# An attention and expert block on one core: tiles normalised inside the attention steps, and linear-attention states added from PSUM

## The reference

```python
xn = layernorm(x)
q, k, v = xn @ Wq, xn @ Wk, xn @ Wv          # 16 heads of 16
# heads 0..3: softmax attention over the own window of 128 tokens and the one before it, causal
# heads 4..15: linear attention, in blocks of 64 tokens
q = softmax(q); k = elu(k) + 1
ctx = cumsum(k^T v over blocks) / (cumsum(sum of k) + 1e-6)     # of the blocks before
out = q @ ctx
attn = concat(local, out) @ Wo + bo
# experts: 8 of them, each token goes to the two with the best scores xn @ router_w.T
h = gelu(xn @ w1[e].T); y += gate * (h @ w2[e].T)               # 256 -> 1024 -> 256
return x + attn + y
```

## Time and profile before

| | us |
|---|---|
| median of 3 runs | 804.63 (802.73 to 806.93) |
| the profiled execution | 808.07 |
| its span, first to last instruction | 806.3 |
| PE busy | 688.7 (85%) |
| DVE, ACT, POOL busy | 464.5, 403.9, 411.5 |

### The profile page before, as it was taken

How to read it: one execution, slowest core, us unless ns; L and a number is a source line. 1 busy time by engine, 2 the same in 40 slices (tenths; PEclk the granted TensorE clock), 3 DMA queues, 4 the chain that set the end, 5 groups by cost and what they waited for, 6 DMA issues and landing times.

```text
span 806.3 us, 21562 instructions
## 1 busy us (share of the span) xinstructions
PE 688.7 (85%) x6874; PEld 542.5 (67%) x6875; DVE 464.5 (58%) x1600; ACT 403.9 (50%) x1128; POOL 411.5 (51%) x429
## 2 busy tenths in 40 slices
PE   1689999999558686887589999999999999999883
PEld 1456666666335454554378888888888888888763
DVE  5789899887788878787532344344433333333331
ACT  4568888888335454555243344444334433343331
POOL 5647777767434344347224555555554555444522
PEclk9989999999767777788799999999999999999998
DMA  8034343343111312122124444444444444443421
GB/s 267 8 132 133 119 143 109 107 128 104 65 48 47 74 53 66 54 80 52 43 51 69 74 78 77 79 77 77 74 77 74 75 74 75 74 71 58 63 43 20
DMA packets 87991, 64.26 MB, mean 80 GB/s; under 512 B 54675, under 2 KB 81556, under 8 KB 87924
## 3 DMA queue, kind: packets, MB, share of 16 engines
q1 hardware_dynamic: 73204, 43.69, 20.0%
q0 software_dynamic: 13632, 18.91, 15.4%
q10 hardware_dynamic: 1088, 0.79, 0.3%
HBM read 36.08 MB, written 17.96 MB: 67 GB/s over the span
## 4 chain that ended last, share of the span: by engine, by line
PE 49%; issue 21%; POOL 18%; DVE 6%; SPq 2%; DMA 2%; ACT 1%; POOLq 0%; DVEq 0%
PE bank L283 25%; PE bank L1198 21%; POOL stage L837 3%; SPq L689 2%; POOL xb L830 2%; POOL ke L817 2%; POOL w2l L839 2%; POOL cum L828 2%; POOL w1l L839 2%; POOL atl L824 1%; POOL rows L744 1%; POOL rstd L799 1%; DMA stage<-xin 1%; DVE stats L1225 1%; DVE w1h L1238 1%
## 5 line engine op out<-in xcount | busy, mean ns | idle before, releaser
L283 PE MATMUL bank<-stage,w1h 128*128 128x256 f16 (+1 forms) x1248 | 198.1, 266 | 6.5 <-DMA stage<-xin 5.1
L283 PE MATMUL bank<-stage,w1l 128*128 128x256 f16 (+1 forms) x624 | 164.0, 265 | 0.0
L1198 PE MATMUL bank<-w2h,pt 128*128 x568 | 154.9, 273 | 5.9 <-issue 4.8
L1198 PE MATMUL bank<-w2h,spare 128*128 x568 | 154.8, 273 | 0.0
L1198 PE MATMUL bank<-w2l,pt 128*128 x568 | 154.8, 273 | 0.0
L283 PEld LDWEIGHTS bank<-stage,w1h 128*128 x1248 | 114.5, 98 | 26.9 <-issue 9.3
L1020 ACT ACTIVATE pt<-ss 128x512 f16<-128x512 f32 (+1 forms) x78 | 41.8, 583 | 149.1 <-PE bank L1198 149.1
L872 POOL DMA_INDIRECT out<-attn,rows_to x35 | 59.0, 1685 | 74.9 <-DMA out<-attn,rows_to 48.7
L872 POOL DMA_INDIRECT out<-res,rows_to x36 | 57.6, 1600 | 70.1 <-DMA stage<-rows 50.7
L824 POOL TENSOR_TENSOR atl<-attn,ath 128x128 f16<-128x128 f32 x32 | 13.7, 427 | 150.1 <-ACT ath L956 150.1
L1013 ACT ACTIVATE ss<-bank 128x512 f32<-128x512 f32 (+1 forms) x78 | 42.2, 548 | 69.7 <-remote 59.3
(11 more groups left out here) (249 smaller groups left out, 1673.1 us busy)
## 6 DMA issues: line engine op xcount, KB each, us to landing
stage<-w1c SPq DMA_DIRECT2D x16, 512.0 KB, 3.7
stage<-w2c SPq DMA_DIRECT2D x16, 512.0 KB, 3.8
xb<-x SPq DMA_DIRECT2D x32, 128.0 KB, 3.6
out<-res SPq DMA_DIRECT2D x32, 128.0 KB, 3.5
stage<-xin SPq DMA_TRANSPOSE x144
stage<-rows SPq DMA_TRANSPOSE x140
w1h<-x SPq DMA_DIRECT2D x8, 256.0 KB, 4.3
xin<-x SPq DMA_DIRECT2D x16, 128.0 KB, 3.8
```

The lines of the kernel that those rows point to most:

```text
L283: ins = pe.matmul(dst, lhs(a, k), rhs(c, k), start=(n == 0), stop=(n == len(terms) - 1))
L1198: ins = pe.matmul(bY[h][:, 0:D], (hh, hl)[a][:, f, h * P:(h + 1) * P], (w2h, w2l)[c][:, DS(which * (FC * D) + f * D, D)], start=(f == a == ...
```

## The change

- Eight tiles (four pairs, `AHEAD` = 4) are normalised in the head, with the weights after the second pair and POOL's constants ahead of its first `rstd_of`. The other 24 go by pairs in the steps: statistics and scaling at steps 0 to 11 (`early(0)`), lower halves a step later (`early(1)`), turning two later (`early(2)`), the router three later. x and the split rows live in 8 slots, loaded and stored pair by pair.
- The contexts of both sequences stay in one bank, `b_state`; DVE adds a block's context from PSUM to the raw state (`raw`), once for each block of 64 tokens, in different parts of the step. POOL multiplies both raw states by the mask into `state`, and TensorE's linear rows wait for that.
- q isn't divided by its sums; DVE multiplies the linear rows by the reciprocals while it takes them out of PSUM (`lrow`), as the first operation of its step.
- `rrec` moves to the end of DVE's step, the copy of `pt` goes to ACT from step 14 on, routing starts at step 14, and one-hot columns come 6 to a step (11 steps), in two parts.

```diff
-CH = 8
+CH = 6
-LEAD = 16
-AHEAD, WEIGHTS_AT = LEAD // 2, 3
+AHEAD, WEIGHTS_AT = 4, 2
+SLOTS = 8
...
+            def early(self, lag):
+                q = AHEAD + self.t - lag
+                return (2 * q, 2 * q + 1) if AHEAD <= q < PAIRS else ()
...
-        BATCHES = NT * TOPK // CH
-        SCORED = NT + 2 - LEAD
+        BATCHES = -(-NT * TOPK // CH)
+        SCORED = PAIRS - 1 - AHEAD + 3
+        ACT_TURNS = SCORED
```

SP, in its step:

```diff
-                    if t.early(LEAD - 2):
-                        ...
-                        sp.dma_start(xn_rows[...], rows[b][:, 0:D])
-                    if t.t and t.early(LEAD + 1):
-                        t.wait(s["xs_in"], LEAD - 1)
-                        load_x(t, LEAD + 1)
+                    if t.early(2):
+                        store_rows(t.early(2)[0] // 2)
+                    if SLOTS + t.t < PAIRS:
+                        sp.wait_ge(s["rl_in"], 2 * t.t + 2)
+                        load_x(SLOTS + t.t)
```

POOL, in its step (`ke` stands first, `lo` last, as before):

```diff
                         t.wait(s["pr_ps"], -4)
                         pool.tensor_tensor(atl[b][:, 2 * P:3 * P], ...)
-                        t.wait(s["new_in"], -2)
-                        t.wait(s["att_ps"], -2)
-                        pool.tensor_tensor(cum[b][:], cum0[b][:], new1[b][:], ALU.add)
                         pool.tensor_tensor(xb[b][:], xb[b][:], bias[:], ALU.add)
-                    if t.early(LEAD - 1):
-                        lower_half(t.t + LEAD - 1)
+                    for u in t.early(1):
+                        lower_half(u)
                     if t.has(0):
                         pool.tensor_scalar(stage[m][:], stage[m][:], WS, 1.0, ...)
+                    if t.has(-1):
+                        t.wait(s["state1_in"], -1)
+                        t.wait(s["lin_ps"], -3)
+                        pool.tensor_tensor(state[b][:], raw[b][:], ctx_mask[:].unsqueeze(1).to_broadcast([P, 2, CTX]),
+                                           ALU.mult).then_inc(s["mask_in"], 1)
```

TensorE:

```diff
                         t.wait(s["qgt_in"], -2)
-                        halves_ = [(slice(0, 64), cum[b]), (slice(64, P), cum0[b])]
+                        t.wait(s["mask_in"], -2)
+                        halves_ = [(slice(0, 64), state[b][:, 0, :]), (slice(64, P), state[b][:, 1, :])]
...
                     scores_of(t, 1)
+                    if t.early(2):
+                        pe.wait_ge(s["rl_in"], t.early(2)[1] + 1)
+                        pe.wait_ge(s["xt_in"], t.early(2)[0] + 1)
+                        turn_x(t.early(2)[1], b_xnt)
...
+                        if t.has(0):
+                            t.wait(s["state0_in"], 0)
+                        add_to_state(t, 0)
...
+                    if t.has(-1) and t.has(1):
+                        t.wait(s["state1_in"], -1)
+                        add_to_state(t, 1)
```

DVE:

```diff
+                    if t.has(-2):
+                        t.wait(s["lin_ps"], -2)
+                        t.wait(s["att_ps"], -3)
+                        dve.tensor_tensor(heads(lrow[:]), heads(b_att[:, 0:D]), spread(qrec[b][:], DH), ALU.mult)
+                    if t.has(0):
+                        ...
+                            t.wait(s["ctx1_ps"], -2)
+                            t.wait(s["mask_in"], -2)
+                            dve.tensor_tensor(raw[b][:, 0, :], b_state[...], raw[b][:, 1, :], ALU.add)
...
-                        dve.tensor_tensor(new0[b][:], b_ctx[:, D:D + CTX], ctx_mask[:], ALU.mult)
-                        dve.tensor_tensor(new1[b][:], b_tok1[:, D:D + CTX], ctx_mask[:], ALU.mult)
-                        dve.reciprocal(rden[b][:, :, 0], cum[b][:, 0:CTX:CTX - 1])
-                        dve.tensor_tensor(cum0[b][:], cum[b][:], new0[b][:], ALU.add)
+                        t.wait(s["ctx0_ps"], -1)
+                        dve.tensor_tensor(raw[b][:, 1, :], b_state[...], raw[b][:, 0, :], ALU.add)
...
-                        dve.tensor_tensor(heads(qs[b][:, 0:GD]), heads(qs[b][:, 0:GD]), spread(qrec[b][:], DH), ALU.mult)
+                    if t.has(-1):
+                        t.wait(s["prob1"], -1)
+                        t.wait(s["att_ps"], -3)
+                        dve.reciprocal(rrec[b][:], rsum[b][:])
```

ACT:

```diff
-                    if t.has(-2):
-                        act.activation(lrow[:], b_att[:, 0:D], ACT.Copy)
...
+                        if half_ == 0 and t.early(2):
+                            copy_turned(t.early(2)[1], b_xnt)
...
+                        if t.t >= ACT_TURNS:
+                            act.activation(pt[:, 0:2, :, :], b_s[0][:]..., ACT.Copy)
...
+                    for u in t.early(0):
+                        ...
+                        upper_half(u)
```

More of the change, by code:

```diff
@@ L111, in block_kernel @@
         negmax, rsum, rrec = pair("negmax", [P, LH]), pair("rsum", [P, LH]), pair("rrec", [P, LH])
-        cum, cum0 = pair("cum", [P, CTX]), pair("cum0", [P, CTX])
-        new0, new1 = pair("new0", [P, CTX]), pair("new1", [P, CTX])
+        state = pair("state", [P, 2, CTX])
+        raw = pair("raw", [P, 2, CTX])
         rden = pair("rden", [P, 2, 2])
@@ L777, in constants @@
                         step += 1
+                    for b in range(2):
+                        pool.memset(raw[b][:, 0, :], 0.0).then_inc(raw_zero, 1)
                     pool.memset(sm["one"], 1.0)
@@ L1040, in _ @@
                 pe.wait_ge(pool_first, 3)
-                for t in range(LEAD):
+                for t in range(2 * AHEAD):
                     pe.wait_ge(s["rl_in"], t + 1)
@@ L1078, in step @@
                     t.wait(s["res_in"], -4)
-                    if t.early(LEAD - 3):
-                        router_of(t.t + LEAD - 3)
+                    for u in t.early(3):
+                        router_of(u)
                     if t.t == RANKS:
@@ L1306, in step @@
                         route_rows(dve)
-                    if t.has(-2):
-                        b = t.row(-2)
-                        t.wait(s["prob1"], -2)
-                        dve.reciprocal(rrec[b][:], rsum[b][:]).then_inc(s["rrec_in"], 1)
-                    if t.early(LEAD):
-                        u = t.t + LEAD
-                        dve.wait_ge(x_loaded[u % 2], 16 * ((u - LEAD) // 2 + 1))
-                        mean_of(xin[u % 2][:, 0:D], u)
-                        variance_of(u)
-                        guarded(u, 1)
+                    if t.early(0):
+                        begin(t.early(0)[0] // 2)
+                    if HOT <= t.t < HOT + BATCHES:
+                        route_onehots(dve, t.t - HOT, 0, 3)
                     if t.has(-1):
@@ L1331, in step @@
                         b = t.row(-1)
-                        t.wait(s["ctx_ps"], -1)
-                        t.wait(s["cum_in"], -3)
-                        dve.tensor_tensor(new0[b][:], b_ctx[:, D:D + CTX], ctx_mask[:], ALU.mult).then_inc(s["new0_in"], 1)
-                        dve.tensor_tensor(new1[b][:], b_tok1[:, D:D + CTX], ctx_mask[:], ALU.mult).then_inc(s["new_in"], 1)
-                        dve.reciprocal(rden[b][:, :, 0], cum[b][:, 0:CTX:CTX - 1])
-                        t.wait(s["new0_in"], -1)
-                        dve.tensor_tensor(cum0[b][:], cum[b][:], new0[b][:], ALU.add).then_inc(s["cum0_in"], 1)
-                    if t.has(-1):
-                        b = t.row(-1)
-                        t.wait(s["cum0_in"], -1)
-                        dve.reciprocal(rden[b][:, :, 1], cum0[b][:, 0:CTX:CTX - 1]).then_inc(s["rden_in"], 1)
-                    if t.early(LEAD):
-                        t.wait(s["rl_in"], LEAD - 2)
-                        scaled(xin[t.row(LEAD)][:, 0:D], t.t + LEAD)
+                        t.wait(s["ctx0_ps"], -1)
+                        dve.tensor_tensor(raw[b][:, 1, :], b_state[:, b * CTX:(b + 1) * CTX], raw[b][:, 0, :], ALU.add)\
+                           .then_inc(s["state1_in"], 1)
+                        t.wait(s["state1_in"], -1)
+                        dve.reciprocal(rden[b][:].rearrange("p g u -> p u g"), raw[b][:, :, 0:CTX:CTX - 1])\
+                           .then_inc(s["rden_in"], 1)
+                    for u in t.early(0):
+                        scaled(u)
+                    if HOT <= t.t < HOT + BATCHES:
+                        route_onehots(dve, t.t - HOT, 3, CH)
                     if t.has(0):
@@ L1378, in step @@
                                                  op0=ALU.mult, op1=ALU.subtract).then_inc(s["kt_in"], 1)
-                    if t.has(-1):
+                    if t.has(-1) and t.t < ACT_TURNS:
                         t.wait(s["pt_ps"], -1)
```

244 lines of the change are left out of this document (120 added, 124 removed).

## The result

| | before | after |
|---|---|---|
| median, us | 804.22 (802.73 to 806.93, 4 runs) | 829.08 (828.77 to 835.22, 4 runs) |
| ratio of after to before | | 1.032 (95% interval 1.027 to 1.038) |
| the profiled execution, its span | 808.07, 806.3 | 835.22, 833.4 |

The change makes the kernel 25 us slower. The profiled execution after is the longest of its four, 6 us over the median (the span of another one was 826.9), so stages read from it can hold up to 6 us too much between them.

What follows compares the result with a forecast made beforehand. A new loop (TensorE's linear rows, VectorE's masks, ACT's last local piece, POOL's mask) bounds each step: 50.6 + 10 x 13.4 + 19 x 10.2 + 22, tail and experts unchanged, +20 us: 825 us, range 799 to 843.

Steps and rivals of the forecast that it cites:

- The mask: POOL's multiplication of both states (128x388), last in its stretch before TensorE's linear rows: 1.0 us, between 0.73 and 1.2.
- A doubled step at full clock: Steps 1 to 12, with two tiles a step: 10.2 + 1.28 + 0.60 + 0.38 + 0.1 = 12.6 us.
- L to M: From TensorE's linear rows to the start of VectorE's masks: 3.77 us plain; doubled steps add 0.38 and 0.1.
- M to L957: From VectorE's masks to the end of ACT's last local piece: 3.19 us plain, 0.60 more in doubled steps.
- The clock: TensorE's clock falls after a 3.1 us wait: 1.8 us in half of ten doubled steps, 13.4 on average.
- rival 2: The clock falls at every doubled step: 14.4 us each, 834 us, to 843 if plain steps fall too; chance 0.14.
- Rival 1: TensorE keeps its clock: ten doubled steps at 12.6 us, falls after routing half as dear, 815 us; chance 0.2.
- The head: Before step 0, half as many tiles: step 0 12 us sooner; ramp +3; step 3's linear rows at 50.6.
- L(13): Start of TensorE's linear rows of step 13: 184.6 us, from 147.5, after ten steps of 13.4.
- From L(13) to L(32): Between TensorE's linear rows of steps 13 and 32: 19 x 10.2 us, plus 22 for routing, clocks, table, gathers.
- The one-hot steps: VectorE's work falls to about 8 us, so the loop over POOL decides: 13.6 becomes about 10.6 us.
- Rival 3: POOL's stretch before the linear rows isn't on the loop's end: 758 us, or 790 to 800 if partly true; chance 0.17.

Runs made afterwards that it cites:

- dummy matmuls: Changed kernel with 40 matmuls of 124 columns to unused columns, ahead of TensorE's wait for the mask in steps 3 to 14: 813.22 us, ratio 1.011.

## Why the prediction was right, and where not

Forecast: 825 us, slower; measured: 829.08. The mechanism is the one it names, and its place is shown from both sides: one POOL operation moved within the loop takes off 47 us, one added puts 29 on. The terms, one by one:

- **The mask** was taken at 1.0 us between 0.73 and 1.2; it takes 0.93 to 0.95.
- **A doubled step at full clock** was 12.6. With the dummy matmuls it is 12.23: L to M 4.14 for 3.77 + 0.38 + 0.1, M to L957 3.66 for 3.19 + 0.60, POOL 4.43 for 3.24 + 1.28. Each is 0.09 to 0.13 below its term.
- **The clock** is where the step's size failed. The prediction took the fall in half of the ten steps at 1.8 us, 0.9 on average; it comes in every one, at 1.5. That the step is near all the same, 13.76 for 13.4, is in part luck: its terms at full clock were 0.3 too dear, and the fall 0.6 too cheap. So rival 2's premise was right and its price of 14.4 too high. The rule of the Trainium skill (TensorE: Matmul & The Clock Gate, HAM oscillation), that such an engine falls back in every round, agrees with these steps; the page tells it of an engine that waits for a DMA between its bursts. The prediction put the wait at 3.1 us, between one of 2.13 that kept the clock and one of 3.32 that lost it; it is 2.60, and loses it. The two rows couldn't settle this, as they show only the matmuls right behind a wait. In the kernel before the clock was down 1.6 us ahead of the matmuls at 267.77, while behind those at 370.18 it stayed at 1.00 to 372.0 and was then at 0.50, TensorE being idle again since 371.3; and in the kernel after it falls 1 us behind the wait. Rival 1, the clock kept, is what the run with dummies makes of the kernel: 813 us for its 815.
- **The head** was put at L(3) = 50.6, and is 45.7. Step 0 starts at 23.4 for 24, so the ramp is what was too dear: no 3 us more, and not at a low clock (1.00 there, where the earlier trace rows has 0.85).
- **L(13)** at 183.3 for 184.6: 4.9 less in the head, 3.6 more in ten steps.
- **From L(13) to L(32)** it is 224.7 us for 215.8. Against 19 steps of 10.2 the 22 us extra became 30.9: three routing steps +20.9 for the 16 allowed, the two steps with gathers +6.7 for 3, steps 13 and 14 +2.5, for which nothing was allowed, and the twelve steps from L(18) +0.8 for 3. This is the term that was mis-sized most. The prediction gave routing 3 us of slack on VectorE and didn't follow its own remark that the rows' product is now first in VectorE's step: behind a block it holds TensorE's projection and, through it, the scores. In the kernel before `rrec` held TensorE in the same place, so the comparison of old and new routing hid it. Up to 6 us of this stage may be the profiled execution's own. Two kernels with the same routing, profiled within 1.5 us of their medians, narrow that down: their three routing steps take 50.2 us (dummy matmuls) and 50.5 (six pairs ahead) for 51.5, so about +20 of the +20.9 is real; their two steps with gathers take 24.0 and 24.4 for 27.1, which is +3.6 to +4.0 for the 3 allowed. Why those two steps are longer in some kernels is open.
- **The one-hot steps** came to 10.25 us for 10.6, near enough, and that the loop over POOL decides there is right. What held them at 13.6 before was given wrongly: "That is the gain" was said of VectorE's busy time, with the division's 1.64 us at its head. The division alone, taken from the kernel before, made it slower. What the runs show to matter is `rrec` ahead of the one-hots (which the prediction mentions in one sentence, at no price, and which alone is worth 23 us, 14.7 of them here) and the one-hots cut into two parts, most of which fall where POOL is idle (40 us if undone). With `rrec` early VectorE is full at 11.8 us a step, so for the rest of the way to 10.25 its work does count: the division, the copy of `pt` given to ACT, and twelve one-hot operations in place of sixteen. What each of these is worth there wasn't tried. The same rows gave it away: VectorE was busy 11.05 us in steps of 13.64, so it wasn't full, and TensorE waited for it all the same.
- **Rival 3** is refuted for this kernel and describes its cure. It needed POOL's stretch 0.7 us a step shorter; with the mask behind xb the stretch loses stage and the lower halves, 2.3 us in doubled steps, and stage alone, 1.0, in the others, and the kernel is at 782, between its 758 and its 790 to 800.

## What to carry to other kernels

When a change hands an operation to another engine and makes the next stage wait for it, write down what that engine does between its last release and the operation, and put the operation ahead of what isn't waited for: here its place was worth 47 us, and its own time is 30 us in all (32 times 0.93). Then look at what the rest of that engine's work falls beside: one place further forward the mask gave all but 10 us of it back, in the one-hot steps. Ask of a small operation that others wait for what stands ahead of it in its queue: 0.16 us of work behind a block cost 23 us. And an engine's busy time in a step that is longer than it says only that something else orders the step; start from the wait, not from the sum. A wait isn't yet a price either: with routing moved, 13.6 us of TensorE's waits were exchanged for others, and the median gained 2.

## What the runs showed that was not expected

- VectorE's operations on fp16 tiles in SBUF, 0.24 to 0.30 us by themselves, took 0.94, 1.08 and 2.13 beside POOL operations of 0.94, 1.04 and 2.12. The f32 division of two SBUF tiles took 1.64 us in the one-hot steps and 0.69 with `rrec` early, where less of POOL's work fell beside it. The rows' product and the addition of the states, which read PSUM, kept their 0.42 and 0.35 us beside a POOL operation of 2.13 (289.49 and 289.83 us in the kernel after).
- Added POOL work of 0.72 us a step cost 1.07 us a step on average (29 / 27), and 40 matmuls that compute nothing gave back 15 us.
- Waits of 2.60 us, once a step of 13.8, brought the clock to half speed every time, about 1 us after TensorE had gone on; waits of 1.2 us in steps of 10.25 never did.
